# Attention edges of a graph network: two stores of 16 tiles per group, and all source indices loaded in two transfers

## What is computed

```python
def gat_layer(h, src, dst, W, al, ar, b):
    feat = (h @ W).reshape(n, H, F)
    el = jnp.sum(feat * al[None], axis=-1)
    er = jnp.sum(feat * ar[None], axis=-1)
    e = jax.nn.leaky_relu(el[src] + er[dst], NEG_SLOPE)
    m = jax.ops.segment_max(e, dst, num_segments=n)
    ex = jnp.exp(e - m[dst])
    denom = jax.ops.segment_sum(ex, dst, num_segments=n)
    a = ex / denom[dst]
    msg = feat[src] * a[:, :, None]
    out = jax.ops.segment_sum(msg, dst, num_segments=n)
    out = out + b.reshape(1, H, F)
    return jax.nn.elu(out).reshape(n, H * F)
```

## Time and profile before

| | |
|---|---|
| median of 3 runs | 8319.48 us |
| profiled execution, own time | 8387.07 us |
| its span | 8385.4 us |
| DVE busy | 5316.5 us (63%) |
| POOL busy | 5471.9 us (65%) |
| ScalarE busy | 2244.0 us (27%) |
| TensorE busy | 2488.6 us (30%) |

### The profile page before, as it was taken

How to read it: one execution, slowest core, us unless ns; L and a number is a source line. 1 busy time by engine, 2 the same in 40 slices (tenths; PEclk the granted TensorE clock), 3 DMA queues, 4 the chain that set the end, 5 groups by cost and what they waited for, 6 DMA issues and landing times. The chain is left out here.

```text
span 8385.4 us, 59216 instructions
## 1 busy us (share of the span) xinstructions
PE 2488.6 (30%) x11337; PEld 1707.7 (20%) x11337; DVE 5316.5 (63%) x9727; ACT 2244.0 (27%) x5114; POOL 5471.9 (65%) x5324
## 2 busy tenths in 40 slices
PE   5777777667777676000000000004100000000000
PEld 4444444444444455000000000003100000000000
DVE  6777777667777767556556655653456555655656
ACT  3666666656666552000000000002000000000002
POOL 4777767667777546666666666646756666666664
PEclk8888889888888888555555555557555555555555
DMA  7555555555555447556555655643556555655556
GB/s 231 163 158 167 162 161 169 152 151 164 163 164 164 142 136 214 175 178 197 187 187 182 195 186 178 197 148 89 154 173 197 187 188 180 194 185 181 191 180 221
DMA packets 791714, 1466.07 MB, mean 175 GB/s; under 512 B 188921, under 2 KB 522174, under 8 KB 791100
## 3 DMA queue, kind: packets, MB, share of 16 engines
q0 software_dynamic: 250192, 671.13, 29.1%
q1 hardware_dynamic: 541420, 793.88, 27.3%
HBM read 752.61 MB, written 713.36 MB: 175 GB/s over the span
## 5 line engine op out<-in xcount | busy, mean ns | idle before, releaser
L1816 POOL DMA_INDIRECT gb_g<-table,ix_g x3126 | 2963.9, 948 | 1491.8 <-issue 940.1
L585 POOL DMA_INDIRECT gb<-table,src x1563 | 1877.4, 1201 | 757.2 <-issue 478.1
L1922 DVE SCALAR_TENSOR_TENSOR gb_g<-gb_g,same_g,wv 128x256 f32<-128x256 f32 x3024 | 1449.4, 479 | 1234.3 <-DVE gb_g L1922 537.7
L1096 PE MATMUL pm<-ident,tl 128*4 128x128 f32 x2 | 0.7, 372 | 4625.0 <-DMA tl<-sums 4625.0
L619 PE MATMUL po<-parts,sel 128*128 128x256 f32 x3930 | 1051.1, 419 | 557.6 <-ACT ost L685 342.0
L1849 ACT ACTIVATE ww<-ee 128x132 f32<-128x132 f32 (+3 forms) x102 | 28.5, 280 | 4130.4 <-DVE ee L1900 2548.4
L1910 DVE TENSOR_TENSOR wv<-gb_g,ww 128x1024 f32<-128x1024 f32 x782 | 955.1, 1221 | 0.0
L619 PEld LDWEIGHTS po<-parts,sel 128*128 128x128 f32 x3930 | 780.4, 207 | 809.2 <-issue 543.5
L1096 PEld LDWEIGHTS pm<-ident,tl 128*4 128x4 f32 x2 | 0.2, 82 | 4625.9 <-DMA tl<-sums 4625.9
L762 DVE TENSOR_TENSOR pt<-gb,pt 128x256 f32<-128x256 f32 x392 | 167.4, 427 | 610.2 <-ACT pt L679 459.2
L679 ACT ACTIVATE pt<-pt,sh 128x128 f32<-128x128 f32 x1568 | 436.9, 344 | 333.0 <-remote 200.4
(11 more groups left out here) (302 smaller groups left out, 4197.2 us busy)
## 6 DMA issues: line engine op xcount, KB each, us to landing
sums<-gb_g SPq DMA_DIRECT2D x780, 528.0 KB
sums<-ost SPq DMA_DIRECT2D x393, 512.0 KB
gb_g<-table,ix_g POOLq DMA_INDIRECT x3126
gb<-table,src POOLq DMA_INDIRECT x1563
table<-f SPq DMA_DIRECT2D x48, 520.0 KB
x<-in_x SPq DMA_DIRECT2D x50, 256.0 KB
at<-in_rbf SPq DMA_DIRECT2D x100, 128.0 KB
hT_d<-hT SPq DMA_DIRECT2D x49, 256.0 KB
```

Source lines behind the costliest of these rows:

```text
L585: eng.indirect_dma_start(out=gb[:, group(k), half(k) + j, 0:4, :].rearrange("p a c -> p (a c)"), out_offset=None, in_=q.table0[:, :], in_o ...
L1816: eng.indirect_dma_start(out=gb[:, p, j, 0:FR], out_offset=None, in_=q.table1[:, :], in_offset=bass.IndirectOffsetOnAxis(ap=ix[:, p, j:j + ...
L1922: ins = eng.scalar_tensor_tensor(rows[:, t0 + t, 0:D], row, same[:, t:t + 1], wv[k % 2][:, j, :], ALU.mult, ALU.add)
```

## The change

SP's eight stores per group of four tiles become two of 16 tiles, the first when four quads are done and the second at the group's end. The index tile `ix` holds all 1563 columns of a layer, loaded in two transfers: group 0, and all the rest; POOL waits for them at groups 0 and 1 alone. POOL's gathers of all groups are written out in place of the loop of three groups, since each now reads its own columns of `ix`, and the empty instruction behind its waits is gone. Of the four end pieces the first three are stored whole and the last by quads. DVE, ScalarE and TensorE code is as before.

```diff
-        ix = sb(c, f"ix_g{n}", [P, B, SBT], I32)
+        ix = sb(c, f"ix_g{n}", [P, CE], I32)
-        s_ix = [Signal(q.sem(nm(f"ix{p}")), inc=16) for p in range(B)]
+        s_ix = [q.sem(nm(f"ix{x}")) for x in range(2)]
-        s_st = [Signal(q.sem(nm(f"st{p}")), per=NQ, inc=16, ahead=1) for p in range(B)]
+        s_st = [Signal(q.sem(nm(f"st{p}")), per=2, inc=16, ahead=1) for p in range(B)]
+        stores = lambda x, t0, t1: [(ts, k + 1) for k, ts in enumerate(quads(t0, t1))] if x == len(ENDS) - 1 else [(slice(t0, t1), len(quads(t0, t1)))]
...
-                def indices(s, p):
-                    eng.dma_start(ix[:, p, :], a["src_chunks"].rearrange("p (s t) -> s p t", t=SBT)[s, :, :]).then_inc(s_ix[p].sem, 16)
-                def body(s, p, more):
-                    if more:
-                        eng.wait_ge(s_g[p].sem, s_g[p].at(s // B))
-                        indices(s + B, p)
+                def body(s, p):
                     eng.wait_ge(s_seg.sem, s_seg.at(s))
-                    for k, ts in enumerate(quads(0, SBT)):
-                        eng.wait_ge(s_sum.sem, s_sum.at(s, k + 1))
-                        eng.dma_start(out_v[:, s * SBT + 4 * k:s * SBT + 4 * k + 4, :], gb[:, p, ts, :]).then_inc(s_st[p].sem, 16)
+                    for ts, done in ((slice(0, SBT // 2), NQ // 2), (slice(SBT // 2, SBT), NQ)):
+                        eng.wait_ge(s_sum.sem, s_sum.at(s, done))
+                        eng.dma_start(out_v[:, s * SBT + ts.start:s * SBT + ts.stop, :], gb[:, p, ts, :]).then_inc(s_st[p].sem, 16)
...
-                for p in range(B):
-                    indices(p, p)
+                for x, ts in enumerate((slice(0, SBT), slice(SBT, CE))):
+                    eng.dma_start(ix[:, ts], a["src_chunks"][:, ts]).then_inc(s_ix[x], 16)
...
-                    eng.wait_ge(s_ix[p].sem, s_ix[p].at(i))
+                    if s < 2:
+                        eng.wait_ge(s_ix[s], 16)
                     eng.wait_ge(s_st[p].sem, s_st[p].at(i, back=1))
                     eng.wait_ge(s_sum.sem, s_sum.at(s, 1, back=2))
-                    eng.nop(nofuse=True)
...
-                with eng.Fori(0, LOOPS) as i:
-                    for p in range(B):
-                        whole(i, p)
-                for p in range(B - 1):
-                    whole(LOOPS, p)
+                for s in range(SB - 2):
+                    free(s, s // B, s % B)
+                    for j in range(SBT):
+                        rows(s, j, s % B, s_g[s % B].sem)
```

More of the change, by code:

```diff
@@ L1777, in _ @@
             def _(eng):
-                def indices(s, p):
-                    eng.dma_start(ix[:, p, :], a["src_chunks"].rearrange("p (s t) -> s p t", t=SBT)[s, :, :]).then_inc(s_ix[p].sem, 16)
-                def body(s, p, more):
-                    if more:
-                        eng.wait_ge(s_g[p].sem, s_g[p].at(s // B))
-                        indices(s + B, p)
+                def body(s, p):
                     eng.wait_ge(s_seg.sem, s_seg.at(s))
-                    for k, ts in enumerate(quads(0, SBT)):
-                        eng.wait_ge(s_sum.sem, s_sum.at(s, k + 1))
-                        eng.dma_start(out_v[:, s * SBT + 4 * k:s * SBT + 4 * k + 4, :], gb[:, p, ts, :]).then_inc(s_st[p].sem, 16)
+                    for ts, done in ((slice(0, SBT // 2), NQ // 2), (slice(SBT // 2, SBT), NQ)):
+                        eng.wait_ge(s_sum.sem, s_sum.at(s, done))
+                        eng.dma_start(out_v[:, s * SBT + ts.start:s * SBT + ts.stop, :], gb[:, p, ts, :]).then_inc(s_st[p].sem, 16)
                 def end(x, s, t0, t1):
                     eng.wait_ge(s_seg.sem, s_seg.at(SB - 2 + x))
-                    for k, ts in enumerate(quads(t0, t1)):
-                        eng.wait_ge(s_sum.sem, summed(x) + k + 1)
+                    for ts, done in stores(x, t0, t1):
+                        eng.wait_ge(s_sum.sem, summed(x) + done)
                         eng.dma_start(out_v[:, s * SBT + ts.start:s * SBT + ts.stop, :], gb[:, s % B, ts, :]).then_inc(s_st[s % B].sem, 16)
@@ L1804, in _ @@
                 for s in range(SB - 2):
-                    body(s, s % B, s + B < SB)
+                    body(s, s % B)
                 for x, e in enumerate(ENDS):
                     end(x, *e)
-                eng.wait_ge(s_st[0].sem, s_st[0].at(SB // B, sum(len(quads(t0, t1)) for s, t0, t1 in ENDS if s == SB - 1)))
-                for p in range(1, B):
-                    eng.wait_ge(s_st[p].sem, s_st[p].at(SB // B - 1))
+                for p in range(B):
+                    eng.wait_ge(s_st[p].sem, s_st[p].base + 16 * (sum(2 for s in range(SB - 2) if s % B == p)
+                                                                 + sum(len(stores(x, t0, t1)) for x, (s, t0, t1) in enumerate(ENDS) if s % B == p)))
                 eng.wait_ge(s_none, 48)
@@ L1814, in _, with rows @@
             def _(eng):
-                def rows(j, p, signal):
+                def rows(s, j, p, signal):
                     eng.indirect_dma_start(out=gb[:, p, j, 0:FR], out_offset=None, in_=q.table1[:, :],
-                                           in_offset=bass.IndirectOffsetOnAxis(ap=ix[:, p, j:j + 1], axis=0)).then_inc(signal, 16)
+                                           in_offset=bass.IndirectOffsetOnAxis(ap=ix[:, s * SBT + j:s * SBT + j + 1], axis=0)).then_inc(signal, 16)
                 def free(s, i, p):
@@ L1821, in free @@
                         eng.wait_ge(s_held, H * SPANS)
-                    eng.wait_ge(s_ix[p].sem, s_ix[p].at(i))
+                    if s < 2:
+                        eng.wait_ge(s_ix[s], 16)
                     eng.wait_ge(s_st[p].sem, s_st[p].at(i, back=1))
                     eng.wait_ge(s_sum.sem, s_sum.at(s, 1, back=2))
-                    eng.nop(nofuse=True)
                 eng.indirect_dma_start(out=ini[:, :], out_offset=None, in_=q.er_d, in_offset=col(q.chunk_node, 0)).then_inc(s_ini, 16)
-                def whole(i, p):
-                    free(i * B + p, i, p)
+                for s in range(SB - 2):
+                    free(s, s // B, s % B)
                     for j in range(SBT):
-                        rows(j, p, s_g[p].sem)
-                with eng.Fori(0, LOOPS) as i:
-                    for p in range(B):
-                        whole(i, p)
-                for p in range(B - 1):
-                    whole(LOOPS, p)
+                        rows(s, j, s % B, s_g[s % B].sem)
                 for x, (s, t0, t1) in enumerate(ENDS):
@@ L1841, in _ @@
                     for j in range(t0, t1):
-                        rows(j, s % B, s_ge[x])
+                        rows(s, j, s % B, s_ge[x])
             @block.scalar
```

## The result

| | before | after |
|---|---|---|
| median | 8320.76 us (4 runs, 8296.06 to 8346.87) | 8447.04 us (4 runs, 8416.62 to 8454.16) |
| profiled execution, span | 8385.4 us | 8442.6 us |

The changed kernel is slower: ratio 1.0153, 95% interval 1.0127 to 1.0178. The forecast was 8145 us with a range of 7950 to 8450 us. Its sign was wrong; the time lies next to that of rival C (8450 us), which had 25%.

The account below looks back on a forecast made before the run. The slow gait in two attention edge phases bounds the kernel; 46.1 to 44.2 us per group, 47 groups, 2 layers, gains 175 us off 8387, less 68 us profiling excess: 8145 us, range 7950 to 8450.

Parts of the forecast that it names:

- rival C: Edge phases: fast stretch of about 40 us makes pauses too short; 47.0 us per group, 60 to 80 us more per layer; 25%.
- (b): Fast stretch near a layer's end, POOL in straight code: 44 us, 35 gathers, about 13 stores.
- the two gaits: DVE in the edge phases: quads of 3.07 us fast, 7.00 us slow, with equal instruction times; late semaphore updates blamed.
- Stores: cost 0 by their landing: Larger stores land in 8.8 us and some 2 us more, before the first quad's update releases POOL; cost 0.
- Indices and POOL's written-out code: cost 0: Later index load covered by late gathers; straight POOL code still issues a gather every 1.25 us; both cost 0.
- Rivals A and B: A: slow gait never returns, 7720 us, 15%. B: nothing changes, stretches stay 30 us, 8320 us, 15%.
- I take 50 us: Fast stretch after POOL's restart in the changed kernel, chosen between bounds of 44 and 63 us; 44.2 us per group.
- my lower bound of 44 us: Shortest fast stretch expected after the change, from (b); it would give 45.3 us per group and a gain of 75 us.
- The 68 us taken off the profiled time: Whole kernel: the profiled execution lies 68 us over the median, so 8212 us became 8145 us.
- The backlog of updates with one drain: Edge phases: semaphore updates, 16 per transfer, fill a backlog of 268 against a drain of 9.2 per us, bringing the slow gait.
- (a): Usual fast stretch from POOL's restart to the first late row sum: 30 us, 24 gathers, about 10 stores.
- (c): Fast stretch at the layer's start: 63 us, 50 gathers, 3 stores; taken as the upper bound.

Follow-up runs that it names:

- The hold: Changed kernel, POOL also waiting after five tiles of each group until DVE has done the first quad of the group before; 8277.67 us, ratio 0.9859.
- the small loads: Changed kernel with six added loads of 1 KB per group that nothing reads; 8404.23 us, ratio 1.0015.
- later release: Kernel before, POOL waiting for the fifth quad of group s-2 in place of the first; 8398.66 us, ratio 1.0102.
- hold after six: Changed kernel, POOL also waiting after six tiles of each group until DVE has done the first quad of the group before; 8316.06 us, ratio 0.9904.

## Why the prediction was wrong

One line of the kernel before is needed here beside its rows: the restart of POOL from which stretch (b), near the layer's end, is counted:

```profile
5425.91 0.95 POOL L1816 DMA_INDIRECT gb_g<-table,ix_g  x1 [12.07 <-DVE wv L1910]
```

- *What bounds the kernel, and the two gaits: right.* Gathers stay at 1.25 us, instruction times didn't move, the slow quad stayed at 7.0 us. The hold shows it the other way round: with the slow gait gone, 1187 us of idle time ahead of row sums go.
- *Stores: cost 0 by their landing, right.* POOL's long waits name the product on DVE only, never a store.
- *Indices and POOL's written-out code: cost 0, right beside eight stores* (0.9986 [0.9968, 1.0004] without the stores' part), *wrong beside two:* 17 to 31 us per layer more than with the stores alone.
- *The slow gait comes later, not never: right.* Rivals A and B are out.
- *"I take 50 us": the step that failed.* The stretch is 41.3 us. It lies under my lower bound of 44 us, and that bound was read wrongly, twice. First the number: POOL restarts at 5425.9 and the first late row sum starts at 5471.16, which is 45.3 us, not the 44 us of the window that I had taken. Then the reason. I took this long stretch at the layer's end, (b), for a bound because POOL runs straight code there. But DVE and ScalarE leave their loops at the same place. In the changed kernel POOL is straight everywhere, the usual stretch is 41 us, and (b) is still 46 us in the second layer; with the two other loops written out nearly every stretch is 45 us. Loops on engines that I had not listed were the difference.
- *What follows from a stretch of 40 us: the cycle of rival C, right.* It forecast 47.0 us per group, and the cycle shown has 47.2; pauses of 2 to 4 and 17 us forecast, 1.8 and 19.7 us measured there (the idle times of its rows less the 0.3 us between any two gathers). Between groups 2 and 44 POOL's pace is 47.1 us per group against 46.2 before. The pause that DVE needs to return to the fast gait was put at 9 us; the trace with the small loads puts it between 7.5 and 7.8 us, with only the two exceptions named against it.
- *Rival C's price of 60 to 80 us per layer: wrong by its own numbers.* (47.0 - 46.1) x 47 groups is 42 us per layer, or some 8405 us in all, and the profiled layers show just that, 39 and 48 us. That the median came so near to 8450 us is in part luck: 39 of its 126 us are not in the layers that were profiled.
- *The gain at the lower bound: not borne out.* For a stretch of 44 us the sum gave 45.3 us per group and 75 us of gain. With stretches of 45.5 us (loops written out) the pauses were mostly 17 to 19 us and not 16, the pace 46.1 us, and the layers took 2300 and 2296 us against 2295 and 2296 before.
- *The 68 us taken off the profiled time: not borne out.* The profiled execution of the changed kernel (8444.56 us) is 2.5 us under its median. Without this term the forecast was 8212 us.
- *The backlog of updates with one drain: fell.* Fitted to (a) and (c) it was r = 9.2 per us and 268 deep. The kernel before with the later release runs fast through 54 transfers, 864 updates, in 50.5 us; that leaves 864 - 465 = 399, half as much again as fits. The number of transfers does count (35.3 us with small ones added), but so does what came before the restart. My second theory, a budget of 53 transfers given back in the pause, held for the hold after five on the changed kernel and failed for the hold after six, for the kernel before with the hold and for the stretches of 52 us.
- *The range* reached 8450 and so just held 8447. The chance given to C (25%) was too small for a turning point that lay between the two measured stretches, 30 and 45 us.

**What stays open.** Which unit holds the updates back, what it counts, and why the same kernel runs fast for 41 or 61 us depending on whether POOL restarts 3 or 15 us into DVE's quads. No view of the trace shows a queue of updates, so the backlog is a picture and not a finding; what is shown is how stretches and pauses answer to the stores, to the small loads and to the waits. That a pause of 5 us in each group keeps the slow gait away is shown; why 3.9 us does not is not.

That the recording of an execution itself brings the slow gait was given no weight in the prediction, since the timed runs were 68 us shorter than the profiled one. This does not rule it out. Each timed run on record has a span and a granted clock of its core as well, so it may have been recorded too, and the kernel before differs by 81 us between chips (8310 and 8391 us). No run is known to be free of it. Nor is it known where those 81 us arise, since no trace of the kernel before was kept on the faster chip.

## What to carry to other kernels

Where two engines run in a cycle of fast and slow stretches, a small lengthening of the fast one can turn the cycle over to a worse one; before estimating the gain, ask at which size the next pause becomes too short to do its work. Here the cycle was cured at the wait that places the pause, not at the load: one wait of 5 us in each group gained 0.95% on the kernel before (34 to 36 us per layer), and some 2% on the changed one (8450 to 8278 us on two chips, 95 to 109 us per layer). And a stretch of the trace may serve as a bound only when every engine's code there has been compared, not just that of the engine under change.

## What was not expected of the hardware

- One more wait in each group made the kernel faster and POOL's waits shorter in all: they add up to 671.9 us in 58 pauses after the change, 511.2 us in 94 with the hold; many short pauses keep the slow gait away where few long ones only end it.
- A few tenths of a microsecond decide: in one trace every pause of POOL of 7.8 us or more brought the fast gait back, and none of up to 7.5 us did.
- The form of the code (a loop or written out) on DVE and ScalarE changed how long the fast gait lasts, at the same instructions: from 41 to 45 us with POOL released by the first quad, from 61 to 52 us with the fifth.
- Transfers of 1 KB, six per group, took 6 us off the fast stretch; stores of 2112 KB, two per group in place of eight of 528 KB, added 9 to 11 us to it.
